# Score slots and maximum items over both array halves and two banks, drained by one instruction

## What is computed

```
sim = jnp.einsum('bhid,bhjd->bhij', q, k) * scale
a = jax.nn.softmax(sim, axis=-1)
out = jnp.einsum('bhij,bhjd->bhid', a, v)
out = out.transpose(0, 2, 1, 3).reshape(b, n, heads * dh)
return out @ wo + bo
```

## Time and profile before

| | us |
|---|---|
| median of 3 runs | 925.96 |
| lowest, highest | 920.62, 926.14 |
| the profiled execution, its time | 923.25 |
| its span, first to last instruction | 921.3 |

### The profile page before, as it was taken

The page is one execution under the profiler, slowest core; times in us unless marked ns, Lnnn a source line. Parts: engine busy times, 40 slices in busy tenths (PEclk is TensorE's granted clock), DMA queues, the critical chain, the costliest instruction groups (busy, mean ns, idle before and its releaser), DMA issues.

```text
span 921.3 us, 21210 instructions
## 1 busy us (share of the span) xinstructions
PE 880.2 (96%) x7810; PEld 594.2 (64%) x7810; DVE 669.9 (73%) x1607; ACT 654.7 (71%) x1423; POOL 55.3 (6%) x92
## 2 busy tenths in 40 slices
PE   8999999999999999999999999999999999999987
PEld 6656565666666577676667776665676666766655
DVE  3978878878788876657566667776777898686822
ACT  7677786877777777667777576676777777776652
POOL 2000000000000000000000000000000000000100
PEclk9999999999999999999999999999999999999999
DMA  8111121111111201001000300001102111111100
GB/s 292 43 36 36 36 47 24 24 29 24 27 44 33 47 22 26 19 18 36 13 1 2 124 3 2 22 11 28 30 19 47 36 32 28 31 36 24 31 9 7
DMA packets 25964, 32.21 MB, mean 35 GB/s; under 512 B 9220, under 2 KB 17416, under 8 KB 25608
## 3 DMA queue, kind: packets, MB, share of 16 engines
q1 hardware_dynamic: 25864, 30.86, 13.1%
HBM read 9.21 MB, written 0.66 MB: 11 GB/s over the span
## 4 chain that ended last, share of the span: by engine, by line
PE 79%; DVE 8%; ACT 8%; issue 4%; ACTq 0%; DVEq 0%
PE pv_ps L1010 17%; PE bank_ps L952 12%; PE bank_ps L972 11%; PE bank_ps L928 8%; PE bank_ps L929 7%; DVE mx L1428 5%; PE bank_ps L1057 5%; PE bank_ps L986 4%; ACT probs L1259 3%; PE bank_ps L1037 3%; PE bank_ps L1130 3%; PE bank_ps L1118 2%; PE bank_ps L1174 2%; ACT oT L1268 1%; PE bank_ps L1076 1%
## 5 line engine op out<-in xcount | busy, mean ns | idle before, releaser
L1428 DVE TENSOR_REDUCE mx<-bank_ps 128x1 f32<-128x512 f32 (+3 forms) x720 | 452.1, 682 | 91.0 <-PE bank_ps L972 89.6
L1259 ACT ACTIVATE probs<-bank_ps 128x512 f32<-128x512 f32 x736 | 380.9, 601 | 116.7 <-PE bank_ps L952 115.2
L1010 PE MATMUL pv_ps<-probs,v 128*9 128x256 f32 (+2 forms) x2944 | 199.3, 376 | 5.4 <-ACT probs L1259 2.3
L952 PE MATMUL bank_ps<-qT,ring 64*128 64x256 f32 x1280 | 171.0, 303 | 2.5 <-DVE gate L1515 1.0
L972 PE MATMUL bank_ps<-ring,qT 64*128 64x512 f32 (+1 forms) x800 | 168.4, 393 | 2.4 <-ACT kdense L1310 1.1
L952 PEld LDWEIGHTS bank_ps<-qT,ring 64*128 64x128 f32 x1280 | 128.6, 185 | 62.7 <-issue 22.3
L972 PEld LDWEIGHTS bank_ps<-ring,qT 64*128 64x128 f32 x800 | 87.3, 184 | 43.2 <-issue 19.6
L1010 PEld LDWEIGHTS pv_ps<-probs,v 128*9 128x9 f32 (+2 forms) x2944 | 57.4, 90 | 76.4 <-issue 22.7
L1310 ACT ACTIVATE kdense<-bank_ps 128x512 fp32r<-128x512 f32 (+2 forms) x116 | 58.3, 556 | 22.2 <-PE bank_ps L1057 21.8
L1234 ACT ACTIVATE ks<-bank_ps 128x320 fp32r<-128x320 f32 x80 | 35.7, 447 | 42.5 <-PE bank_ps L929 22.1
L1452 DVE TENSOR_TENSOR qT<-bank_ps,qT 128x256 fp32r<-128x256 f32 (+1 forms) x108 | 47.0, 436 | 23.6 <-PE bank_ps L986 23.2
(11 more groups left out here) (178 smaller groups left out, 1037.1 us busy)
## 6 DMA issues: line engine op xcount, KB each, us to landing
ring<-kdense SPq DMA_DIRECT2D x240, 64.0 KB, 2.0
ring<-kdense SPq DMA_DIRECT2D x160, 32.0 KB, 1.9
wb<-in_w_blk SPq DMA_DIRECT2D x2, 2240.0 KB, 8.4
wd<-in_w_down SPq DMA_DIRECT2D x2, 400.0 KB, 8.5
x<-in_x SPq DMA_DIRECT2D x4, 160.0 KB, 4.5
bias<-in_bias SPq DMA_DIRECT2D x1, 640.0 KB
out_rows<-x SPq DMA_DIRECT2D x4, 160.0 KB, 1.9
gate<-in_ctx SPq DMA_DIRECT2D x3, 192.0 KB, 4.8
```

The costliest lines, as they stand in the source:

```text
L952: mm = pe.matmul(bank[0:kr, i * a["nq"]:(i + 1) * a["nq"]], key_op(n, h)[:, c * P:c * P + kr], query_rows(u, b, h), start=True, stop=True)
L1010: mm = pe.matmul(pv_ps[32 * j:32 * j + a["dh"] + 1, 0:a["nq"]], v, probs[0:kr, s % N_P, i * a["nq"]:(i + 1) * a["nq"]], start=(c == 0), st ...
L1259: nc.scalar.activation(probs[0:kr, s % N_P, 0:w], bank[0:kr, 0:w], ACT.Exp, scale=float(a["dh"]) ** -0.5).then_inc(free, 1)
L1428: nc.vector.tensor_reduce(mx[b][0:rows, t, heads[0]:heads[-1] + 1:heads[-1] - heads[0] or 1], bank[0:rows, 0:a["hpm"] * a["nk"]].rearrange ...
```

## The change

A slot now holds the four heads of a quad for one chunk: 368 slots instead of 736. An item holds the same tile and head position of both halves: 360 instead of 720. Both write two neighbouring banks, half 0 to the first and half 1 to the second, with the matmuls of the halves in turn. One exponential or one reduction reads both banks (1024 columns instead of 512) and raises one semaphore. The eight banks become three pairs (`pair_ps`), one single (`lone_ps`) and `pv_ps`. Slots and items take a pair; all other steps take any one of the seven banks, by preference the single or one whose neighbour is in use (`alone`). A pair is waited for at up to two owners (`owners`). `probs` keeps its size as N_D = 4 places of two. The lanes of the planner advance together, and the due times, which count in slots, are halved (FIRST_W goes from 3 to 2, BG_LEAD from 11 to 6). In the SP queue the load of the last context rows moves from the `ca_q` step to its `low` step. The matmuls, their shapes and their number are the same. The diff, with its context and repeating parts left out:

```diff
@@ -63,14 +63,16 @@
+N_D = 4
+N_PAIR = 3
-PV_LAG = 2
-FIRST_W = 3
-K_LEAD = 4
-TAIL = 40
-BG_LEAD = 11
-M_LEAD = 8
+PV_LAG = 1
+FIRST_W = 2
+K_LEAD = 2
+TAIL = 20
+BG_LEAD = 6
+M_LEAD = 4
@@ -117,8 +119,7 @@
-    per = [[(t, rows, hs[i:i + a["hpm"]]) for i in range(0, 2, a["hpm"]) for t, rows in tiles] for hs in same_half(u, qd)]
-    return [item for both in zip(per[1], per[0]) for item in both]
+    return [(t, rows, i, [hs[i:i + a["hpm"]] for hs in same_half(u, qd)]) for i in range(0, 2, a["hpm"]) for t, rows in tiles]
@@ -206,8 +207,7 @@
-                        for k, heads in enumerate(same_half(u, qd)):
-                            slots.append(dict(n=n, u=u, b=b, c=c, heads=heads, last=c == n_c - 1 and k == 1))
+                        slots.append(dict(n=n, u=u, b=b, c=c, heads=same_half(u, qd), last=c == n_c - 1))
@@ -309,13 +309,13 @@
-        return 0.455 * rows, [("dve", 60 + 1.05 * rows)]
+        return 0.455 * rows, dve(2 * rows)
-        return 0.458 * a["hps"] * a["nq"], act(a["hps"] * a["nq"])
+        return 0.458 * a["hps"] * a["nq"], act(2 * a["hps"] * a["nq"])
@@ -529,24 +525,31 @@
                 else:
-                    free = seen = max(self.clock["pe"], self.lanes[side] if shape == "rows" else max(self.lanes))
+                    free = seen = max(self.lanes)
                 if banks:
-                    open_at = [(0 if self.banks[i] is None else self.at(self.banks[i]), i) for i in banks]
-                    open_at = [x for x in open_at if x[0] is not None]
+                    open_at = [(max(0 if self.banks[j] is None else self.at(self.banks[j]) or LATE for j in banks_used(step, i)), i) for i in banks]
+                    open_at = [x for x in open_at if x[0] < LATE]
                     ready = [x for x in open_at if x[0] <= max(start, seen)]
-                    t, bank = max(ready) if ready else min(open_at)
+                    t, bank = max(ready, key=lambda x: (self.alone(x[1], max(start, seen)), x)) if ready else min(open_at)
+        def alone(self, i, t):
+            if i >= 2 * N_PAIR:
+                return True
+            other = self.banks[i ^ 1]
+            return other is not None and (self.at(other) or LATE) > t
             _, start, free, home, step, bank = choice
-            _, pe, after, shape, side, lock, _, _ = facts(step)
+            _, pe, after, shape, lock, _, _ = facts(step)
@@ -571,7 +571,8 @@
-                self.banks[bank] = ("low", step) if step[0] in LOW else step
+                for j in banks_used(step, bank):
+                    self.banks[j] = ("low", step) if step[0] in LOW else step
@@ -611,12 +612,18 @@
-BANKED = SPARE | {"st", "max"}
+DOUBLE = {"st", "max"}
+BANKED = SPARE | DOUBLE
-    return range(N_BANK) if step[0] in BANKED else ()
+    return range(0, 2 * N_PAIR, 2) if step[0] in DOUBLE else range(N_BANK) if step[0] in BANKED else ()
+def banks_used(step, i):
+    return (i, i + 1) if step[0] in DOUBLE else (i,)
@@ -656,8 +663,14 @@
-            turn[step] = (place[step], uses[place[step]])
-            uses[place[step]] += 1
+            b = place[step]
+            turn[step] = (b, uses[b])
+            uses[b] += 1
+            fills[b] += 2 if step[0] in DOUBLE else 1
+            full_at[step] = fills[b]
+            owners[step] = [user[j] for j in banks_used(step, b) if j in user]
+            for j in banks_used(step, b):
+                user[j] = step
@@ -668,7 +681,13 @@
-        bank_ps = [ctx.enter_context(nc.psum_tensor(f"bank_ps{i}", [P, 512], F32)) for i in range(N_BANK)]
+        pair_ps = [ctx.enter_context(nc.psum_tensor(f"pair_ps{i}", [P, 2, 512], F32)) for i in range(N_PAIR)]
+        lone_ps = [ctx.enter_context(nc.psum_tensor(f"lone_ps{i}", [P, 512], F32)) for i in range(N_BANK - 2 * N_PAIR)]
+        bank_ps = [pair[:, i, :] for pair in pair_ps for i in range(2)] + [lone[:, :] for lone in lone_ps]
+        def bank_of(step):
+            return pair_ps[place[step] // 2] if step[0] in DOUBLE else bank_ps[place[step]]
@@ -725,6 +744,7 @@
+        pair_probs = probs[:, :, :].rearrange("p (n s) w -> p n s w", s=2)
@@ -918,10 +938,9 @@
-                    b, k = turn[step]
-                    if k:
-                        pe.wait_ge(bank_taken[b], k)
-                    return bank_ps[b], bank_full[b]
+                    for owner in owners[step]:
+                        taken(pe, owner)
+                    return bank_of(step), bank_full[place[step]]
@@ -948,16 +967,19 @@
                         kr = chunk_rows(a["nk"], c)
-                        for i, h in enumerate(sl["heads"]):
-                            mm = pe.matmul(bank[0:kr, i * a["nq"]:(i + 1) * a["nq"]],
-                                           key_op(n, h)[:, c * P:c * P + kr], query_rows(u, b, h),
-                                           start=True, stop=True)
-                        mm.then_inc(full, 1)
+                        for i in range(2):
+                            for k in range(2):
+                                h = sl["heads"][k][i]
+                                mm = pe.matmul(bank[0:kr, k, i * a["nq"]:(i + 1) * a["nq"]],
+                                               key_op(n, h)[:, c * P:c * P + kr], query_rows(u, b, h),
+                                               start=True, stop=True)
+                                if i == 1:
+                                    mm.then_inc(full, 1)
                         a = ATT[u]
-                        t, rows, heads = quads[n]["items"][i]
+                        t, rows, _, heads = quads[n]["items"][i]
@@ -968,11 +990,14 @@
                         tt = 0 if t == TQ else t
-                        for j, h in enumerate(heads):
-                            mm = pe.matmul(bank[0:rows, j * a["nk"]:(j + 1) * a["nk"]],
-                                           query_rows(u, b, h)[:, tt * P:tt * P + rows], key_op(n, h)[:, 0:a["nk"]],
-                                           start=True, stop=True)
-                        mm.then_inc(full, 1)
+                        for j in range(a["hpm"]):
+                            for k in range(2):
+                                h = heads[k][j]
+                                mm = pe.matmul(bank[0:rows, k, j * a["nk"]:(j + 1) * a["nk"]],
+                                               query_rows(u, b, h)[:, tt * P:tt * P + rows], key_op(n, h)[:, 0:a["nk"]],
+                                               start=True, stop=True)
+                                if j == a["hpm"] - 1:
+                                    mm.then_inc(full, 1)
@@ -1004,11 +1029,12 @@
                             kr = chunk_rows(a["nk"], c)
-                            for i, h in enumerate(slots[s]["heads"]):
+                            for k, i in ((0, 0), (0, 1), (1, 0), (1, 1)):
+                                h = slots[s]["heads"][k][i]
                                 mm = pe.matmul(pv_ps[32 * j:32 * j + a["dh"] + 1, 0:a["nq"]], v,
-                                               probs[0:kr, s % N_P, i * a["nq"]:(i + 1) * a["nq"]],
+                                               pair_probs[0:kr, s % N_D, k, i * a["nq"]:(i + 1) * a["nq"]],
@@ -1251,12 +1277,12 @@
                         bank, free = filled(act, step)
-                        if s >= N_P:
-                            act.wait_ge(*used_after[s - N_P])
+                        if s >= N_D:
+                            act.wait_ge(*used_after[s - N_D])
                         w = a["hps"] * a["nq"]
-                        nc.scalar.activation(probs[0:kr, s % N_P, 0:w], bank[0:kr, 0:w], ACT.Exp,
+                        nc.scalar.activation(pair_probs[0:kr, s % N_D, :, 0:w], bank[0:kr, :, 0:w], ACT.Exp,
@@ -1423,10 +1449,11 @@
                         a = ATT[u]
-                        t, rows, heads = quads[n]["items"][i]
+                        t, rows, i, _ = quads[n]["items"][i]
                         bank, free = filled(dve, step)
-                        nc.vector.tensor_reduce(mx[b][0:rows, t, heads[0]:heads[-1] + 1:heads[-1] - heads[0] or 1],
-                                                bank[0:rows, 0:a["hpm"] * a["nk"]].rearrange("p (h k) -> p h k", k=a["nk"]),
+                        qd, hpm = quads[n]["qd"], a["hpm"]
+                        m = mx[b][0:rows, t, 4 * qd:4 * qd + 4].rearrange("p (s j) -> p s j" if a["sr"] == 32 else "p (j s) -> p s j", s=2)
+                        nc.vector.tensor_reduce(m[:, :, i:i + hpm], bank[0:rows, :, 0:hpm * a["nk"]].rearrange("p s (h k) -> p s h k", k=a["nk"]),
...
```

More of the change, by code:

```diff
@@ L247, in plan @@
         lists = before(ph, b)
-        spread(span[k - 1][0] - lead if k else -80, span[k][0] - lead, spread_lists(lists))
+        spread(span[k - 1][0] - lead if k else -40, span[k][0] - lead, spread_lists(lists))
         first = [("k_tr", 0, 0, 1, 2), ("q_tr", 0, 0, 2)] if k == 1 else []
@@ L355 @@
 PATIENCE = 800
+LATE = 10**9
 OTHERS = 0.1
@@ L424, in data_needs @@
             s = step[1]
```

(38 more changed lines are left out.)

## The result

| | before | after |
|---|---|---|
| median | 924.32 us (4 runs) | 936.57 us (4 runs) |
| lowest, highest | 920.62, 926.14 | 934.11, 948.71 |
| profiled execution: time, span | 923.25, 921.3 | 936.88, 935.0 |

The changed kernel is slower: the ratio is 1.0129, 95% interval 1.008 to 1.0178. The run of 948.71 us was in a slower state, with a mean granted clock of 0.975, and is left out of the ratio, which compares the fast runs alone. The prediction was 915 us, 894 to 944, faster. The size lies in the range, the direction is wrong, and the result lies nearest to the rival in which the pairs run out.

The account below looks back on a forecast made before the run. PE, busy 880.2 of 921.3 us, was taken as the bound. 923.25 - 17 (pairs by construction) - 4 (half as many drains) + 7 (three pairs) + 5 (longer holds) = 914, set at 915 us; range 894 to 944.

Parts of the forecast that it names:

- the rival in which the pairs run out: Pool of three pairs: PE finds one or two, stretches hold two pairs, a third of waits lengthen; 956 us; slower, chance 0.27.
- The law of a stretch: Rows work on PE, scores and maxima between other kinds: about 0.20 us to enter and 0.24 for each pair.
- the chain's 5 and 3%: Chain of waits: reduction of the maxima (L1428) 5%, exponential (L1259) 3%, 46 and 28 us; faster drains matter only there.
- Pairs by construction: Rows stretches on PE: 154 odd ones each lose half a pair, 0.12 us; up to 18.5 us off, 17 taken.
- the rival "no change": Half-pair gain given back in 40 more stretches (12 us) and 9 us of waits; 923 to 926; chance 0.20.
- step 1: Pairing slots and items of both halves on PE, so that no half pair remains; 17 us off.
- Half as many drains: Merged reductions and exponentials save 22 us of DVE and 26 of ACT; 4 us off the chain.
- Three pairs and longer holds: PSUM pool: 24 more stretches, 7 us more; pairs held longer while drained, 5 us more.
- the row at 24.15: First rows stretch, eight banks' worth: takes 1.84 us where the law gives 1.16, its eighth item waiting for a bank.
- One wait in twenty: Share of PE's 187 weight-load waits for drains taken to grow by 0.5 us; 5 us more.
- signs of being wrong: Over 350 rows stretches, PE waits for L1428's successor over 0.42 us in the mean, or PE idle above 60 us.
- No part of what follows: TensorE's granted clock, in its highest tenth in all 40 slices, 2.4 GHz, was left out of the forecast.

Follow-up runs that it names:

- partners: Kernel before, planner made to follow each slot or item at once by its other-half partner: 926.55 against 927.54 us; with the last context rows' load later, 924.78 against 927.78.
- neighbours: Kernel before with the partner rule, both banks from one of three neighbouring pairs, two drains each freeing its bank: 966.32 us, ratio 1.0407.
- six banks: Kernel before with six shared banks in place of seven, and the changed kernel's place for the last context rows' load: 953.08 us, ratio 1.0263.
- split drains: Changed kernel in its very order, each exponential and reduction as two instructions of 512 columns, pair freed after the second: 962.06 us, ratio to before 1.0356.
- the half drains in the new order: Changed kernel, each drain reading only its pair's first bank, planner told of the shorter drains and making a new order: 868.34 us, ratio 0.9339.

## Why the prediction was wrong

The ladder, by medians: partners -1 us; neighbours +40; merged drains and an order planned for them -30. That adds up to +9, and the result is +12 (the kernels before of the sessions differ by 3): three terms of which two are far larger than forecast and against each other.

*What bounds the kernel.* PE, as said. The law of a stretch (0.20 and 0.24 for each pair) held in the medians of every kernel looked at. The step that failed is the next: I took idle PE (41 us) and the chain's 5 and 3% for what banks and drains are worth. They say what is left over after the planner has filled every gap with another kind of work. They don't say what it paid for the filling, and that price is entries, odd items and waits inside the stretches.

*Pairs by construction*, 17 us forecast, 0 to 3 measured. The count of 154 odd stretches was right, the price was not: a stretch ends on an odd item where its partner is held up or where another kind of work is worth more at that point, and in before those were most of them. I had given this case as the reason of the rival "no change", and it was the right reading of step 1.

*Half as many drains*, 4 us forecast, 25 measured in a fixed order (11 at full clock). The durations were right, and the busy time saved was for DVE; for ACT it was 18 us, not 26. The price of an us of drain was 0.08 in the forecast and between 0.4 and 0.7 in the runs, 0.2 to 0.4 at full clock. I kept "nothing" and "the 48 us of both engines" as bounds and took the value at the wrong end.

*Three pairs and longer holds*, 7 + 5 us forecast, 40 measured with two drains left (30 at full clock). This is the term that turned the sign. The bounds were 23 and 94 us, and the row at 24.15 had shown 0.7 us of wait when the pool ran out. "One wait in twenty" had no row behind it. The number of waits for drains did not rise much; who waited for the reduction in the changed kernel, for the earlier trace rows:

```profile
PEld pair_ps L973: 14.0, 32
PEld pair_ps L996: 11.6, 23
PE pair_ps L996: 4.7, 10
PE pair_ps L973: 2.6, 8
```

Only rows work waits longer now (32.9 us here against 19.1). The signs of being wrong came true in two of three: 357 stretches (over 350) and, narrowly, 0.44 us for a wait of the weight loads for the reduction (31.7 us in 72 waits; over 0.42), while PE's idle time, 56.9 us, stayed under 60. The rest shows as shorter stretches: the planner avoids the wait and pays an entry, 120 times.

*The rivals.* "The pairs run out" was the mechanism: stretches of 2.04 pairs in the mean (two in the rival), 357 of them (over 350 was the sign). Its sum of 956 had only 4 us for the merged drains, and 17 for pairs by construction that the runs did not show. Its rule from the Trainium skill (Perfetto Trace Analysis, Optimizing Scalar/DVE Operations), that breaking up instructions may help where ScalarE and VectorE are not saturated, did not hold here: broken up, the same order took 25 us more, at 69 and 70% busy. That run gives the rule no full chance, as both parts hold the pair to the end; the neighbour run, where each part frees its bank, took longer still (966.32 us), in another order.

*The clock.* "No part of what follows" was wrong. The page's row shows tenths of slices of 23 us and hides a few microseconds at the lower level; each 0.01 of mean clock goes with 9 us.

What stays open: how the 30 us between the neighbour run and the changed kernel divide between the merged drains and the new order, since those two differ in both, in the halved due times and in the place of the last context rows' load; what made up the 20 us of the neighbour rule that are neither entries nor clock; and what the clock does in each order, which was only followed, not set.

## What to carry to other kernels

Where a planner fills every gap, the idle time of the busiest engine prices neither buffers nor drains: one run with a buffer less and one with longer drains in the same order do, and here they gave 26 us for a bank of seven and about a half us for each us of drain (0.2 to 0.4 without the part of the clock), on engines that were busy some 70%. Merging instructions can pay even there, but not if it makes the pool coarser, and unpaired items need not be waste: here a rule that removed them all gained nothing clear of noise.

## What the runs showed of the hardware

- A reduction over two neighbouring banks of PSUM takes 1.22 us for 1024 columns against 0.68 for 512, an exponential 1.03 against 0.61. The slopes of operations within one bank give 1.24 and 1.06, so the step from one bank to the next costs nothing that shows.
- The mean granted clock of one unchanged kernel differed from run to run between 0.984 and 1.0, and the time with it from 937 to 921 us. The idle PE time of a kernel does not settle it: in the profiled executions six banks had 33 us idle by gaps at 0.996 and split drains 58 at 0.973, but the half drains in the new order had only 22 at 0.982. In the run of the partner rule 13.7 us at the lower level began at 325.0, within the gap of 4.5 us (323.3 to 327.8).
- Issuing the halves in turn (two of one, two of the other half, or one by one) made no difference to a stretch: one pair 0.43 us in the median in both forms. Where two slots are issued one behind the other, two matmuls of the first half and then two of the second, the first two starts of such a pair lie 7 ns apart in the median (partner run): the second half's first matmul starts ahead of the first half's second, which was issued before it.
